# Attention: softmax sums from ones columns of V, outputs of a batch packed through a scratch array, maxima split before they are turned

## The reference, cut to what matters

```python
# layer 0
att = jnp.einsum('bthd,bThd->bhtT', q, k) / math.sqrt(HD)
att = jnp.where(causal, -jnp.inf, att)
att = jax.nn.softmax(att, axis=-1)
out = jnp.einsum('bhtT,bThd->bthd', att, v).reshape(Bx, Tx, Cx)
return out @ Wo + bo
```

## Time and profile before

| what | value |
|---|---|
| median of 3 runs | 2572.59 us (2566.7 to 2574.55) |
| the profiled execution | 2572.08 us, its span 2569.4 us |
| PE matmul busy | 2053.6 us, 80% of the span |
| DVE, ACT, POOL busy | 1488.1 us (58%), 1216.8 us (47%), 942.1 us (37%) |
| DMA engines busy, by the queue that carries nearly all | 20.2% |
| mean granted TensorE clock | 0.874 |
| first attention, first A tile to last `ytmp` | about 187 to 644 us |
| second attention, the same | about 1168 to 1681 us |

### The profile page before, as it was taken

One profiled execution on the slowest core, in us unless ns is written; L12 is line 12 of the kernel. 1 busy time (PEld: TensorE's weight loads), 2 busy tenths in 40 slices (PEclk: granted clock), 3 DMA queues, 4 the chain that ended last, 5 costly groups with the idle time before them and its releaser, 6 DMA issues. The chain is left out here.

```text
span 2569.4 us, 47234 instructions
## 1 busy us (share of the span) xinstructions
PE 2053.6 (80%) x14500; PEld 1137.3 (44%) x14500; DVE 1488.1 (58%) x2642; ACT 1216.8 (47%) x2866; POOL 942.1 (37%) x663
## 2 busy tenths in 40 slices
PE   4639999999525726647999999974899999999996
PEld 2314555555424614432333333342555555555552
DVE  3426666664231123326777777524788878877883
ACT  0114555555001301113666666611776767767762
POOL 2322222222131052321222222213766666666660
PEclk9768999999557956656999999956999999999997
DMA  2431212120202242232222222112111111111110
GB/s 86 131 114 53 56 55 58 55 63 29 79 23 81 84 119 77 73 95 73 60 64 69 69 71 63 37 62 82 38 32 41 35 35 41 40 37 53 35 50 19
DMA packets 131137, 156.53 MB, mean 61 GB/s; under 512 B 20064, under 2 KB 87395, under 8 KB 130784
## 3 DMA queue, kind: packets, MB, share of 16 engines
q1 hardware_dynamic: 128992, 151.16, 20.2%
q0 software_dynamic: 2048, 4.16, 0.6%
HBM read 90.54 MB, written 50.07 MB: 55 GB/s over the span
## 5 line engine op out<-in xcount | busy, mean ns | idle before, releaser
L910 DVE TENSOR_REDUCE M_sb<-banks 128x1 f32<-128x512 f32 (+3 forms) x1024 | 561.7, 586 | 327.9 <-PE banks L716 180.9
L825 ACT ACTIVATE probs_sb<-banks 128x512 f32<-128x512 f32 (+3 forms) x1024 | 496.4, 512 | 338.5 <-PE banks L740 164.7
L713 PE MATMUL banks<-K_sb,Q_sb 72*128 72x512 bf16 (+3 forms) x1024 | 362.8, 358 | 80.8 <-DMA V_sb<-v_dram 64.1
L737 PE MATMUL banks<-Q_sb,K_sb 75*128 75x512 bf16 (+3 forms) x1024 | 350.1, 345 | 7.3 <-ACT probs_sb L825 4.2
L871 POOL TENSOR_TENSOR mres_sb<-mneg_sb,mparts_sb 4x512 f32<-4x512 f32 x64 | 73.2, 1144 | 713.5 <-ACT mparts_sb L836 713.5
L713 PEld LDWEIGHTS banks<-K_sb,Q_sb 72*128 72x128 bf16 x1024 | 106.4, 104 | 333.6 <-DVE M_sb L910 205.0
L751 PE MATMUL banks<-probs_sb,V_sb 128*32 128x512 f32 (+3 forms) x2048 | 234.5, 529 | 6.1 <-ACT probs_sb L825 1.4
L1782 ACT ACTIVATE l_p_sb<-banks,l_nb_sb,l_inv_sb 128x128 f32<-128x128 f32 x512 | 228.4, 466 | 12.3 <-DVE l_nb_sb L1954 12.1
L1860 POOL TENSOR_TENSOR l_inv_sb<-l_clip_sb,l_minus_half_sb 128x16 f32<-128x16 f32 x64 | 186.3, 2910 | 57.1 <-DVE l_clip_sb L1929 55.2
L1868 POOL TENSOR_TENSOR l_pn_sb<-l_p_sb,l_rs_sb 128x512 f32<-128x512 f32 x128 | 150.2, 1173 | 154.3 <-DVE l_rs_sb L1960 152.8
L1853 POOL TENSOR_TENSOR l_ts_sb<-l_t_sb 128x1024 f32<-128x1024 f32 x64 | 153.3, 2396 | 41.0 <-DVE l_t_sb L1908 24.2
(11 more groups left out here) (209 smaller groups left out, 4048.8 us busy)
## 6 DMA issues: line engine op xcount, KB each, us to landing
Q_sb<-qk_dram SPq DMA_DIRECT2D x576, 32.0 KB
v_dram<-vpad_sb SPq DMA_DIRECT2D x16, 1024.0 KB, 8.7
V_sb<-v_dram SPq DMA_DIRECT2D x64, 256.0 KB
l_vs_sb<-l_vt_sb SPq DMA_DIRECT2D x112, 128.0 KB, 2.4
qk_dram<-parts_sb SPq DMA_DIRECT2D x96, 128.0 KB
K_sb<-qk_dram SPq DMA_DIRECT2D x96, 96.0 KB
x_norm_sb<-x SPq DMA_DIRECT2D x24, 256.0 KB, 2.7
x<-xnew_sb SPq DMA_DIRECT2D x16, 256.0 KB, 2.1
```

What stands on the lines that cost most here:

```text
L713: mm = pe.matmul(out[:, 0:width], g.Q[0:RK, slot, h, k * P:(k + 1) * P], g.K[0:RK, slot, hk(h), 0:width], start=True, stop=not causal)
L737: mm = pe.matmul(SB[n % 2][:, t0:N], g.K[0:RM, q, hk(h), k * P:(k + 1) * P], g.Q[0:RM, q, h, t0:N], start=True, stop=not causal)
L825: act.activation(g.probs[:, k % 2, h, t0:N], SB[n % 2][:, t0:N], ACT.Exp, scale=scale)\
L910: dve.reduce_max(g.M[:, u % 2, k, h:h + 1], SA[ring % 3][:, 0:width], AX.X).then_inc(s["a_max"], 1)
```

## The change

- V has 8 columns of ones a head where it had one, so a head's 32 output rows hold 8 rows of data and 8 equal rows of sums.
- The selecting matmuls, the small reciprocals, their repetition, the turning back and the product on DVE are gone. Instead SP stores each unit's output (`keep`) to `o_dram`, and once a batch loads it back as two dense 128 x 512 tiles: data and sums (`pack`). DVE takes one reciprocal of 128 x 512, POOL multiplies, PE does one projection.
- `reduce_max` gives negated maxima. POOL splits them before the turn, as 128 x 16 values in four operations; PE turns the three parts with four bfloat16 matmuls; ACT copies 12 x 512; one DMA moves them from SBUF to Q.
- In layer 0 the mask of the B tiles is no longer a matmul. POOL zeroes the future entries of `probs` after the exponential (`mask_future`: one tiny addition and one `affine_select` over 128 x 4 x 128 for each k), and `pv` waits for it.
- The projection's bank goes to the B tiles (three banks), `probs` has four buffers, `pv` of a k is issued after the last B tile of the next k (it was after the second).
- Loads: 5 a unit where it was 13, with a repeated source. Q and K are loaded once the last B tile of the unit before is done; only V waits for `pv`.

```diff
-            pool.memset(g.vpad[:, :, :, D:D + 1], 1.0)
+            pool.memset(g.vpad[:, :, :, D:2 * D], 1.0)
...
+    g.mres = g.sb("mres", [P, CH, UH])
+    g.mcols = g.sb("mcols", [P, CH, PARTS, UH], BF16)
+    g.mrows = g.sb("mrows", [UH * PARTS, N], BF16)
+    g.probs = g.sb("probs", [P, CH, UH, N])
...
-    SA, SB, OB, MB, YB = g.bank[0:3], g.bank[3:5], g.bank[5], g.bank[6], g.bank[7]
+    SA, SB, OB, MB = g.bank[0:3], g.bank[3:6], g.bank[6], g.bank[7]
...
-    LOADS = 13 * 16
+    LOADS = 5 * 16
...
+                    q_src = g.qk_dram[it, 0, q, part].rearrange("d h n -> d (h n)")
                     r = PARTS * part * D
...
+                    sp.dma_start(g.Q[r:r + PARTS * D, slot, :, :].rearrange("r h n -> r (h n)"),
+                                 q_src.unsqueeze(0).broadcast_to([PARTS, D, UH * N])).then_inc(g.loaded[slot], 16)
...
+                    k_src = g.qk_dram[it, 1, q].rearrange("s d h n -> (s d) (h n)")
+                    sp.dma_start(g.K[0:RK, slot, :, :].rearrange("r h n -> r (h n)"),
+                                 k_src.unsqueeze(0).broadcast_to([PARTS, PARTS * D, UH * N]))\
+                        .then_inc(g.loaded[slot], 16)
+                if wait_pv is not None:
+                    sp.wait_ge(s["pv"], wait_pv)
                 sp.dma_start(g.V[:, slot, :, :], g.v_dram[it].rearrange(
                     "c p (u m) -> p c u m", u=UNITS)[:, :, q, :]).then_inc(g.loaded[slot], 16)
...
-                at = i * 4 + u
-                sp.wait_ge(s["mpart3"], at + 1)
-                sp.dma_start(g.m_dram, g.mparts[:, :, :]).then_inc(s["m_stored"], 16)
-                sp.wait_ge(s["m_stored"], at * 16 + 16)
-                sp.dma_start(g.Q[RK:RM, u % UNITS, :, :], g.m_dram.rearrange("h s n -> s h n"))\
-                    .then_inc(s["m_loaded"], 16)
+                sp.wait_ge(s["mrows"], i * 4 + u + 1)
+                sp.dma_start(g.Q[RK:RM, u % UNITS, :, :], g.mrows[:, :]).then_inc(s["m_loaded"], 16)
+
+            def keep(i, u):
+
+                sp.wait_ge(s["o_copied"], i * 4 + u + 1)
+                sp.dma_start(g.o_dram[i * 4 + u], g.osum[:, :]).then_inc(s["o_stored"], 16)
+
+            def pack(i):
+
+                sp.wait_ge(s["o_stored"], i * 4 * 16)
+                rows = g.o_dram.rearrange("(i u) p n -> i u p n", u=UNITS)[i - 1].rearrange("u (h w) n -> (u h) w n", w=VW)
+                sp.dma_start(g.spack[:, :], rows[:, D:2 * D, :]).then_inc(s["sums_packed"], 16)
+                sp.dma_start(g.opack[:, :], rows[:, 0:D, :]).then_inc(s["packed"], 16)
...
-                            sp.wait_ge(s["pv"], i * 16 + 4 * q)
-                        load(i, q + 3)
+                            sp.wait_ge(s["b_scores"], i * 64 + per * q)
+                            load(i, q + 3, i * 16 + 4 * q)
...
+                    if not (first and q == 0):
+                        keep(i, q - 1)
                     u = m_unit(q, first, last)
                     if u is not None:
                         move_max(i, u)
+                    if q == 0 and not first:
+                        pack(i)
...
-                pe.wait_ge(s["a_max"], i * 64 + (u + 1) * per)
-                pe.wait_ge(s["mneg"], 2 * (i * 4 + u))
-                if u >= 2:
-                    pe.wait_ge(s["onorm"], i * 4 + u - 2)
+                pe.wait_ge(s["mpart3"], i * 4 + u + 1)
+                pe.wait_ge(s["mrows"], i * 4 + u)
+                if u == 3:
+                    pe.wait_ge(s["ytmp"], i)
                 for k in range(CH):
-                    mm = pe.transpose(MB[0:UH, k * P:(k + 1) * P], g.M[:, u % 2, k, :], g.ident[:, :])
+                    mm = pe.matmul(MB[0:UH * PARTS, k * P:(k + 1) * P],
+                                   g.mcols[:, k, :, :].rearrange("p s h -> p (s h)"), g.identb[:, :],
+                                   start=True, stop=True, skip_group_check=True)
...
-                if causal:
-                    mm = pe.matmul(SB[n % 2][:, t0:t0 + P], g.identb[:, :], g.mask[:, 1, :], start=False, stop=True)
-                mm.then_inc(s["b_scores"], 1)
+                    pe.wait_ge(s["m_loaded"], (i * 4 + q + 1) * 16)
+                if ring >= 3:
+                    pe.wait_ge(s["exp"], i * 64 + n - 2)
+                elif ring == 0 and (not isinstance(i, int) or i):
+                    pe.wait_ge(s["exp"], i * 64)
+                pe.matmul(SB[ring % 3][:, t0:N], g.K[0:RM, q, hk(h), k * P:(k + 1) * P],
+                          g.Q[0:RM, q, h, t0:N], start=True, stop=True).then_inc(s["b_scores"], 1)
...
-                pe.wait_ge(s["exp"], i * 64 + q * per + (k + 1) * UH)
+                if causal:
+                    pe.wait_ge(s["masked"], i * 16 + q * CH + k + 1)
+                else:
+                    pe.wait_ge(s["exp"], i * 64 + q * per + (k + 1) * UH)
...
+            def out_project(i, mrows):
+                pe.wait_ge(s["onorm"], i)
+                pe.wait_ge(s["mrows"], mrows)
+                pe.matmul(MB[:, :], g.wo[:, layer, :], g.onorm[:, :], start=True, stop=True).then_inc(s["yacc"], 1)
...
-                            if (k, h) == (0, 1) and m is not None:
+                            if (k, h) == (1, 3) and m is not None:
                                 turn_max(i, m)
-                            if h == 1 and k:
+                            if h == 3 and k:
                                 pv(i, q, k - 1)
-                            elif h == 1 and not (first and q == 0):
+                            elif h == 3 and not (first and q == 0):
                                 pv(i, q - 1, CH - 1)
-                            if (k, h) == (0, 3) and not (first and q < 2):
-                                out_project(i, q - 2)
-                            if (k, h) == (2, 0) and not (first and q == 0):
-                                turn_sums(i, q - 1, m)
-                            if (k, h) == (2, 3) and not (first and q == 0):
-                                spread_inverses(i, q - 1)
+                            if (q, k, h) == (1, 2, 2) and not first:
+                                out_project(i, i * 4 + 3)
...
-                if h == 0 and (q * CH + k >= 2 or not isinstance(i, int) or i):
-                    act.wait_ge(s["pv"], i * 16 + q * CH + k - 1)
+                if h == 0 and (q or not isinstance(i, int) or i):
+                    act.wait_ge(s["pv"], i * 16 + q * CH + k - 3)
                 act.wait_ge(s["b_scores"], i * 64 + n + 1)
-                act.activation(g.probs[:, k % 2, h, t0:N], SB[n % 2][:, t0:N], ACT.Exp, scale=scale)\
+                act.activation(g.probs[:, k, h, t0:N], SB[ring % 3][:, t0:N], ACT.Exp, scale=scale)\
                    .then_inc(s["exp"], 1)
...
+            def copy_rows(i, u):
...
+                act.wait_ge(s["m_loaded"], (i * 4 + u) * 16)
+                act.activation(g.mrows[:, :], MB[0:UH * PARTS, :], ACT.Copy).then_inc(s["mrows"], 1)
...
-                act.wait_ge(s["onorm"], i * 4 + q)
+                act.wait_ge(s["o_stored"], (i * 4 + q) * 16)
...
+                            if (k, h) == (1, 1) and not (first and q == 0):
+                                copy_out(i, q - 1)
+                            if (k, h) == (2, 0) and m is not None:
+                                copy_rows(i, m)
...
+                m = g.M[:, u % 2, :, :]
+                pool.wait_ge(s["a_max"], i * 64 + (u + 1) * per)
+                pool.wait_ge(s["max_turned"], at)
+                pool.tensor_tensor(g.mcols[:, :, 0, :], m, g.zero[:, 0:per].rearrange("p (k h) -> p k h", h=UH),
+                                   ALU.add).then_inc(s["mpart1"], 1)
+                pool.wait_ge(s["mpart1"], at + 1)
+                pool.tensor_tensor(g.mres[:, :, :], m, g.mcols[:, :, 0, :], ALU.subtract).then_inc(s["mres"], 1)
                 pool.wait_ge(s["mres"], at + 1)
+                pool.tensor_tensor(g.mcols[:, :, 1, :], g.mres[:, :, :],
+                                   g.zero[:, 0:per].rearrange("p (k h) -> p k h", h=UH), ALU.add).then_inc(s["mpart2"], 1)
                 pool.wait_ge(s["mpart2"], at + 1)
-                pool.wait_ge(s["m_loaded"], at * 16)
-                pool.tensor_tensor(g.mparts[:, 2, :], g.mres[:, :], g.mparts[:, 1, :], ALU.subtract)\
+                pool.tensor_tensor(g.mcols[:, :, 2, :], g.mres[:, :, :], g.mcols[:, :, 1, :], ALU.subtract)\
                     .then_inc(s["mpart3"], 1)
+
+            def mask_future(i, q, k):
+                t0 = first_query(k)
+                pool.wait_ge(s["exp"], i * 64 + q * per + (k + 1) * UH)
+                at = g.probs[:, k, :, t0:t0 + P]
+                pool.wait_ge(s["masked"], i * 16 + q * CH + k)
+                pool.tensor_tensor(g.seen[:, 0:1], g.zero[:, 0:1], g.zero[:, 0:1], ALU.add)
+                pool.affine_select(at, at, [[0, UH], [1, P]], ALU.is_ge, 0.0, base=0, channel_multiplier=-1)\
+                    .then_inc(s["masked"], 1)
+
+            def normalise(i):
```

(56 more changed lines are left out.)

131 lines of the change are left out of this document (32 added, 99 removed).

## The result

The changed kernel takes 2493.76 us (median of 4 runs, 2475.80 to 2496.98); the kernel before, on the same chip, 2573.57 (4 runs, 2566.70 to 2574.72). The ratio is 0.9681 with a 95% interval of 0.9647 to 0.9715: faster by 80 us. The forecast was 175 us faster, and its range ended at 2490, 4 us short. The profiled execution took 2491.64 us (span 2489.9).

A forecast was written before the change was run, and what follows sets the result against it. PE was taken to bound both attentions. Savings of 87 us (layer 1) and 102 (layer 0), less 14 for reciprocal and row-copy waits, starts and ends about 0, made -175 on 2572.08: 2397, said as 2400; range 2335 to 2490.

The forecast's parts named there:

- PE's list: PE's work per unit falls to 8.65 us in layer 0 and 11.45 in layer 1; units take 10.0 and 12.05.
- Mask on POOL: Layer 0: 0.9 us of mask matmuls leave PE; `pv` waits about 0.9 us a unit for a 1.2 us select.
- The slow select: Rival, layer 0: a select of 5 us on POOL makes the kernel slower than before, 2770 us; chance 0.06.
- the mask paces layer 0: Rival: a 2 us select, or a split at its upper bound, gives 12.3 us a unit, 2480 us; chance 0.20.
- Packed tiles: Stored sums and data, loaded back once a batch, arrive before DVE wants them in unit 1: hidden by 1 us.
- PE loses 1.5 us a batch: Layer 1: DVE's 3.4 us reciprocal between unit 1's maxima, about 2 us covered; 7 times, 11 us.
- The same wait: SP: `pack` waits for the fourth store with unit 1's loads behind it; taken at nothing.
- the signs of being wrong: Select above 2 us, A tiles waiting for V or Q, or granted clock in the attentions below 1.00.
- Starts: Start of each attention: five load issues take about 1.9 us where 13 took 4.6, so -2.7 each.
- Ends: End of each attention: 12.4 us from copy through projection after the last `pv`, so +7 each, +14.
- 2445: Rival: the row move comes late, each unit's first B tile waits, up to 45 us more; chance 0.11.
- Gaps close too: Rival: select nearer 0.8 us and engine ties vanish, units of 9.1 and 11.75 us, 2350 us; chance 0.16.

The follow-up runs named there:

- 9: 4 with `pack` in unit 1 behind the row move, the pieces and the steps after them one or two k later: 2413.08 us, ratio 0.9422.
- 11: 9 with layer 0's mask back on PE as matmuls and no select on POOL: 2418.78 us, ratio 0.9408.
- 10: The kernel before with a spare, unused reciprocal of 512 columns on DVE in unit 1 of each batch, 14 in all: 2577.85 us, ratio 1.0048.
- 6: 5 with the reciprocal in one piece, in unit 2: 2459.88 us, ratio 0.9598.
- 4: The changed kernel with the reciprocal in four pieces of 128 columns, moved with all behind it to unit 2: 2455.51 us, ratio 0.9520.
- 5: 4 with `pack` moved from unit 0 to unit 1, behind unit 1's V load and ahead of the row move: 2428.90 us, ratio 0.9458.
- 12: 9 with Q and K of a unit loaded by 12 issues, as in the kernel before, instead of 4: 2409.66 us, ratio 0.9383.
- 8: 5 with layer 0's mask back on PE as matmuls and no select on POOL: 2439.91 us, ratio 0.9521.

## Why the prediction was wrong

The direction, the mechanism of the gain and both unit times were about right; the price of what happens once a batch was not.

- **PE's list, right.** A unit without a stop takes 9.5 us in layer 0 (forecast 10.0) and 12.25 in layer 1 (1307.58 to 1319.83; forecast 12.05). Averaged over 200 us, with the short waits that are left, 9 has 10.25 and 12.6.
- **Mask on POOL, right by errors that cancel.** The select took 637 ns, half of the 1.2 us taken. The forecast had 0.9 us of matmuls leave and 0.9 us of waiting for POOL arrive; that waiting is nearly absent, but only 7 us of the matmuls' 29 came back (11), in part because PE waits more for DVE and ACT without them. The slow select fell: the Trainium skill's figure for branching code on GpSimd ("GPSIMD Engine Reference", section on performance versus the Vector engine) doesn't apply to this instruction, which takes 1.2 ns an element of a partition and not 10. So did the rival in which the mask paces layer 0: PE's weight loads wait for POOL 5.3 us in 300:500. The small splits read 0.22 us as taken.
- **The reciprocal's length, right:** 3353 ns against 3.4 us. The Trainium skill's repeat count of 8 ("VectorE: DVE Perf Modes", the walkthrough of the pipeline) would give an estimated 4.3; the measurement decides.
- **Here it failed: "Packed tiles: copied at 4.3, stored 6.8, loaded 10, while DVE wants them at 11 in unit 1: hidden by 1 us".** Measured from the unit's start they were copied at 4.5, stored by 9.8 and loaded by 13.5, and wanted at 10.9: 2.6 us late. A 256 KB store was taken at the 2.1 to 2.8 us of the earlier trace rows, of other transfers of that size; this one, behind the unit's loads, took 4.7 (the extremes are 2.0 and 6.9):

```profile
o_dram<-osum_sb SPq DMA_DIRECT2D x64, 256.0 KB, 4.7
```

 That row, of the changed kernel's DMA issues, has the count, the size, and the median us from issue to landing.
- **And with it "PE loses 1.5 us a batch" (2 in layer 0).** It lost 47.0 - 38.0 = 9.0 us in layer 0 and 55.2 - 49.0 = 6.2 in layer 1: (9.0 - 2) x 7 + (6.2 - 1.5) x 7 = 82, the 82 us that the two attentions fell short. That it comes out so evenly is chance: units without a stop were 0.5 us faster than forecast in layer 0, some 15 us in all, and 0.2 us slower in layer 1, some 6, and the rest was lost elsewhere, which was not traced. The block alone cost 0.9 us under the old list (10) and 2.2 or more under the new (6, with waits for the rows beside it). What was missing is that a wait in front of a block adds to it once the cover is used up, and that PE then loses its clock. The text named the clock among the signs of being wrong, and gave it no price; none of the rivals had it.
- **The same wait was put at nothing on SP:** "behind it stand the loads for unit 1's call, which wait longer for the B tiles anyway". Once DVE was free, in 4, V came 0.9 to 2.3 us late, and 5 took nearly all of it away.
- **Starts, wrong.** The four issues before V's take 3.2 us (178.01 to 181.17), where the forecast gave 1.9 to all five, since each Q load takes 0.8 us to issue and one of the old 12 takes 0.35. But that is still less than the old 4.6; what made the start late is the time to landing. The first A tile came 6.2 and 8.3 us after V's issue (before: 3.1 and 3.9), and 9.4 and 11.8 us after the first issue (before: 7.7 and 8.0). So +2 and +4 where -2.7 each was forecast. Why the loads land later is open; with the 12 old ones the start is 7.3 us again (12), and over the whole kernel no gain of the merged loads is seen.
- **Ends, right:** 13.2 us from the end of the last `pv` of layer 0 (576.36) to `ytmp` at 589.56, 5.8 before: +7.4, where +7 was forecast.
- **Between the attentions, open.** 14.3 us were lost there (10.4 in 9's profile). 4 are the late start of layer 1; some 7 are one pause in the combine of layer 0's experts, which the change doesn't touch: DVE waits 8.4 us for a load (at 885.41). The profile of 12 has such a pause too, those of 8, 9 and 10 have none. No run tells why.
- **Rivals.** The two whose times lie nearest, 2480 and 2445, are near by their numbers alone: the mask does not pace layer 0, and PE waits for the row move almost nothing in the changed kernel (0.5 us in 200), though in 5 it was this wait that went with the loss of the clock. "Gaps close too" is not seen.

What is shown: the late sums, the block, the late V and the late rows, by runs that take them away one after another (each moves the steps behind them too), ending with 9, where the clock is 1.00 in those windows and the attentions together save 169 of the forecast's 175 us in its profile. By its ratio the whole kernel saves 149. What is argued: how the 8 us of a stop divide into idle time and half clock; no run holds the clock up while PE stands. The best version is 9 (or 12, the same within its interval): 2.6% of the kernel before below the changed kernel by the two ratios, 67 us.

## What to carry to other kernels

When PE's list gets shorter, price again everything that happens once a batch: the cover that hid it was the work that you removed, and follow each transfer from the engine that copies to the one that wants it with the duration that it has behind the queue's other traffic. A small stop of PE can cost twice, and need not every time, so read the granted clock in windows of 2 us behind each stop. Where a DMA waits for something (here `pack` for a store), put it in SP's order where that has long happened, and behind the transfer that the next unit needs first.

## What the hardware showed that was not expected

- The granted clock fell to 0.50 for some 7 us with stops of PE of 4.89 us, of 1.79 and 0.48 us, and of 0.72 and 0.45 us with 0.3 between; with single waits of 0.72 us (267.24) and 0.90 us (358.94) in 9 and of 0.65 us in 10 it stayed at 1.00. In the last two of the three it fell only after PE had begun again. The length of a stop does not settle it: in 11 one wait of 0.80 us (1361.43) went with a fall and five others of 0.80 us between 1210 and 1464 did not, and in 5 a wait of 1.64 us (1471.78) had none. The executions of one kernel differ in it too: the slowest of 9 (2426.92) has a mean clock of 0.851, the others 0.856 to 0.857. The Trainium skill ("TensorE: Matmul & The Clock Gate", part 1) has the same two levels, 1.2 and 2.4 GHz.
- POOL's affine select over 128x512 float32 in place takes 637 ns, half of a product of the same shape (1264 ns).
- The time that SP takes for one DMA issue differs: 0.7 to 0.9 us for the Q and K loads with a repeated source, 0.3 to 0.4 for the 12 that they replace, for V and for the store of the outputs, 0.6 for the packed tiles and 0.8 for the row move, whose sources are not repeated. What sets it is open.
